# One step order for loads, stores and bias tiles in a two-layer mixing kernel

## The reference, cut to what matters

```
rel  = tril(row - col);  nd = log(|c*rel| + 1) / (log(|c*max(rel_max, threshold)| + 1) + eps)
bias = relu(nd * W1 + b1) @ W2 + b2            # 32 hidden values -> 16 channels
y    = x + bias
out  = y @ (w + eye)                            # channels
     + rank two per row    (qw1, qw2) + rank two per column (kw1, kw2)
     + y * qdd (per row) + y * kdd (per column)
```

## Time and profile before

| | |
|---|---|
| median of three runs (lowest, highest) | 977.46 us (973.42, 980.99) |
| profiled execution: time, span | 958.2 us, 956.4 us |
| mean granted TensorE clock | 0.913 |
| PE busy | 751.1 us (79%) |
| DVE busy | 451.8 us (47%) |
| ACT busy, without its DMA issues | 386.0 us (40%) |
| POOL busy | 369.8 us (39%) |
| DMA, packets' time as share of 16 engines: q1 (SyncE), q10 (ScalarE) | 41.5%, 30.9% |
| moved | 149.64 MB, mean 156 GB/s |

### The profile page before, as it was taken

The page is one execution under the profiler, slowest core; times in us unless marked ns, Lnnn a source line. Parts: engine busy times, 40 slices in busy tenths (PEclk is TensorE's granted clock), DMA queues, the critical chain, the costliest instruction groups (busy, mean ns, idle before and its releaser), DMA issues.

```text
span 956.4 us, 39070 instructions
## 1 busy us (share of the span) xinstructions
PE 751.1 (79%) x18210; PEld 551.5 (58%) x18210; DVE 451.8 (47%) x482; ACT 386.0 (40%) x412; POOL 369.8 (39%) x204
## 2 busy tenths in 40 slices
PE   0687465897779857879899989987979679997972
PEld 0255344675657545656557656756557456766972
DVE  7495332375336533456336534553336334662342
ACT  3969223543545415633434335332433334431200
POOL 4545212232223312326456637553446445650000
PEclk9879777899889987989999989998899899998997
DMA  6785587838982999378964998399835996297089
GB/s 135 178 173 106 123 155 159 193 80 202 233 186 58 216 161 196 91 143 188 249 139 82 231 204 177 62 210 187 188 77 112 234 218 149 54 202 148 5 188 168
DMA packets 364286, 149.64 MB, mean 156 GB/s; under 512 B 97372, under 2 KB 363996, under 8 KB 364124
## 3 DMA queue, kind: packets, MB, share of 16 engines
q1 hardware_dynamic: 226528, 80.00, 41.5%
q10 hardware_dynamic: 137596, 67.14, 30.9%
HBM read 77.61 MB, written 69.47 MB: 154 GB/s over the span
## 4 chain that ended last, share of the span: by engine, by line
PE 54%; SPq 14%; DMA 9%; issue 8%; ACTq 6%; DVE 4%; ACT 4%; POOL 0%; DVEq 0%
PE main L679 22%; PE main L668 18%; PE bias L693 14%; SPq L296 9%; DMA mats_a<-a_mats 7%; SPq L287 5%; ACTq L239 5%; DMA homes<-in_x 2%; ACT homes L440 1%; ACT hidden L429 1%; DVE homes L260 1%; ACT homes L456 1%; DVE homes L574 1%; DMA out_mixed<-homes 1%; DVE w_blocks L549 1%
## 5 line engine op out<-in xcount | busy, mean ns | idle before, releaser
L393 POOL TENSOR_TENSOR hidden<-log_table,row_scale 128x1024 f32<-128x1024 f32 x192 | 365.7, 1919 | 486.8 <-PE bias L693 481.1
L679 PE MATMUL main<-homes,mats_b 32*32 32x120 f32 (+1 forms) x9216 | 283.7, 272 | 84.0 <-issue 59.8
L429 ACT ACTIVATE hidden<-hidden,b_col 128x1024 f32<-128x1024 f32 x192 | 219.0, 1148 | 316.6 <-issue 156.4
L679 PEld LDWEIGHTS main<-homes,mats_b 32*32 32x32 f32 x9216 | 256.5, 133 | 151.4 <-issue 113.8
L668 PE MATMUL main<-homes,mats_a 32*32 32x128 f32 x8192 | 267.5, 280 | 63.1 <-DMA mats_a<-a_mats 35.2
L668 PEld LDWEIGHTS main<-homes,mats_a 32*32 32x32 f32 x8192 | 242.3, 131 | 124.1 <-issue 79.2
L592 DVE SCALAR_TENSOR_TENSOR homes<-bias,b_col,homes 64x512 f32<-64x512 f32 (+1 forms) x256 | 185.9, 747 | 134.1 <-PE bias L693 84.9
L693 PE MATMUL bias<-hidden,w_blocks 128*64 128x512 f32 x768 | 211.0, 655 | 24.8 <-ACT hidden L429 15.3
L574 DVE TENSOR_TENSOR homes<-main,homes 128x1024 f32<-128x1024 f32 x128 | 156.8, 1225 | 137.2 <-PE main L668 134.6
L564 DVE COPY homes<-main 128x960 f32<-128x960 f32 x64 | 74.1, 1158 | 211.2 <-PE main L679 211.1
L456 ACT ACTIVATE homes<-main 128x960 f32<-128x960 f32 (+1 forms) x80 | 71.0, 890 | 136.6 <-PE main L679 118.1
(11 more groups left out here) (36 smaller groups left out, 30.1 us busy)
## 6 DMA issues: line engine op xcount, KB each, us to landing
out_mixed<-homes ACTq DMA_DIRECT2D x208, 192.0 KB
homes<-in_x SPq DMA_DIRECT2D x200, 192.0 KB, 6.5
homes<-in_x SPq DMA_DIRECT2D x72, 256.0 KB, 7.1
out_mixed<-homes ACTq DMA_DIRECT2D x64, 256.0 KB
out_mixed<-homes ACTq DMA_DIRECT2D x72, 128.0 KB, 4.5
homes<-in_x SPq DMA_DIRECT2D x136, 64.0 KB
mats_a<-a_mats SPq DMA_DIRECT2D x256, 32.0 KB
b_mats<-homes SPq DMA_DIRECT2D x2, 512.0 KB, 3.4
```

The source lines that it names most:

```text
L393: nc.gpsimd.tensor_tensor(hidden_tile(u, g).rearrange("p (j s) -> p j s", j=ROWS), bass.AP(logs.tensor, logs.offset, [list(logs.ap[0]), [1 ...
L429: nc.scalar.activation(hidden_tile(u, g), hidden_tile(u, g), ACT.Relu, bias=b1_col[:, 0:1])\
L679: mm = pe.matmul(main[of_group(g), i % 2, j * W:j * W + REGION_TILES[k] * ROWS], b_weights(g, C * ROWS + j), y_column(k, g, C * ROWS + j), ...
```

## The change

Four things change together; the work and its data are the same.

- Stores go two blocks a step, four steps a piece (`store_share`, `store_start`, `stores_at`): steps 2 to 5, 6 to 9, 10 to 13, 14 to 17 and 18 to 21, counted from the row stage's first; the last two pieces reach steps 0 to 6 of the next column stage. In the last region it is four blocks a step, two steps a piece.
- Loads of region k + 2's pieces 0 to 4 go two blocks a step from steps 8, 12, 16, 20 and 24 of region k, counted in the same way (`LOAD_STEPS`, `loads_at`), so that 14 of their 40 DMAs lie in the row stage and 26 in the next column stage (before 24 and 16). Piece 5 of region k + 1 goes in two halves at row steps 8 and 9 (6 and 7 in region 0). The wait for the slots stands once a piece (`wait_slots`).
- SyncE's list now runs over steps. A chunk of row matrices comes one step later in it, with the same wait; in the steps of the column stage nothing in it waits for TensorE.
- Bias tile T of the next region comes at step 3 + T * 26 // 14 instead of 1 + 2 * T (for regions of 15), and ScalarE adds the constant half of tile T - 1 at the bias tile T.

```diff
-PORTIONS = (3, 3, 2)
+STORE_SHARE = 2
+LOAD_SHARE = 2
+LAST_LOAD_STEP = {8: 6, 15: 8}
+LOAD_STEPS = (8, 12, 16, 20, 24)
...
-            return 1 + T * (COL_TILES + REGION_TILES[k] - 3) // (REGION_TILES[k + 1] - 1)
+            return 3 + T * (COL_TILES + REGION_TILES[k] - 5) // (REGION_TILES[k + 1] - 1)
...
+        def blocks_of(part, share):
+            return BLOCK_ORDER[part * share:(part + 1) * share]
+
+        def store_share(k):
+
+            return STORE_SHARE if k + 1 < REGIONS else BLOCKS // 2
+
+        def store_start(k, i):
+
+            ready = piece_start(store_pieces(k), i + 1)
+            return ready if i == 0 else max(ready, store_start(k, i - 1) + BLOCKS // store_share(k))
+
+        def since_rows(r, k, s):
+
+            return s - COL_TILES + (COL_TILES + REGION_TILES[r] if k == r + 1 else 0)
+
+        def stores_at(k, s):
+
+            found = []
+            for r in (k - 1, k):
+                if r >= 0:
+                    for i in range(len(store_pieces(r))):
+                        part = since_rows(r, k, s) - store_start(r, i)
+                        if 0 <= part < BLOCKS // store_share(r):
+                            found.append((r, i, part))
+            return found
+
+        def loads_at(k, s):
+
+            found = []
+            for r in (k + 1, k + 2):
+                if 2 <= r < REGIONS:
+                    for i, start in enumerate(LOAD_STEPS):
+                        part = since_rows(r - 2, k, s) - start
+                        if 0 <= part < BLOCKS // LOAD_SHARE:
+                            found.append((r, i, part))
+            return found
...
-                while k + 1 < REGIONS and loaded[k + 1] < 5:
-                    load_x(k + 1, loaded[k + 1])
-                    loaded[k + 1] += 1
...
-                for T in range(REGION_TILES[k]):
-                    v, last = divmod(tile_of(k, T), CHUNK_TILES)
-                    if last == CHUNK_TILES - 1 and v + A_RING < CHUNKS:
-                        load_mats_a(v + A_RING)
-                    if k + 1 < REGIONS and T == min(6, REGION_TILES[k] - 4):
-                        load_x(k + 1, 5)
-                    if k + 2 < REGIONS and T in (7, 10, 13):
-                        load_x(k + 2, loaded[k + 2])
-                        loaded[k + 2] += 1
+                for s in steps(k):
+                    T = s - COL_TILES
+                    if T > 0 or (s == 0 and k):
+                        v, last = divmod(tile_of(k, max(T, 0)) - 1, CHUNK_TILES)
+                        if last == CHUNK_TILES - 1 and v + A_RING < CHUNKS:
+                            load_mats_a(v + A_RING)
+                    if k + 1 < REGIONS and T in (LAST_LOAD_STEP[REGION_TILES[k]], LAST_LOAD_STEP[REGION_TILES[k]] + 1):
+                        part = T - LAST_LOAD_STEP[REGION_TILES[k]]
+                        if part == 0:
+                            wait_slots(k + 1, 5)
+                        load_x(k + 1, 5, blocks_of(part, BLOCKS // 2))
+                    for r, i, part in loads_at(k, s):
+                        if part == 0:
+                            wait_slots(r, i)
+                        load_x(r, i, blocks_of(part, LOAD_SHARE))
...
-                    for r, i, p in portions_at(k, s):
-                        if p == 0:
+                    for r, i, part in stores_at(k, s):
+                        if part == 0:
...
-                        add_const_bias(k + 1, T)
...
+                        if T:
+                            add_const_bias(k + 1, T - 1)
+                        if T + 1 == REGION_TILES[k + 1]:
+                            add_const_bias(k + 1, T)
```

More of the change, by code:

```diff
@@ L239, in store_block @@
             return eng.dma_start(out[0, :, t0:t0 + n, b * W:(b + 1) * W], home_rows(b, mixed_slot(k, T), n))
-        def portion_blocks(p):
-            return BLOCK_ORDER[sum(PORTIONS[:p]):sum(PORTIONS[:p + 1])]
-        def portions_at(k, s):
-            found = []
[L247 to L253, removed]
+        def blocks_of(part, share):
[8 more added lines that the diff above has]
+        def stores_at(k, s):
+            found = []
+            for r in (k - 1, k):
[13 more added lines that the diff above has]
+                            found.append((r, i, part))
             return found
@@ L275, in load_compact, with wait_slots @@
                              vd.rearrange("o (b p) g m -> p (o b) (g m)", p=P)).then_inc(weights_in[part], DMA)
-            def load_x(k, i):
+            def wait_slots(k, i):
                 T, n = piece_start(load_pieces(k), i), load_pieces(k)[i]
@@ L284, in load_x @@
                     sp.wait_ge(out_done[left], times(STORE_PIECES, left, k - 2) * PER_PIECE)
+            def load_x(k, i, blocks):
+                T, n = piece_start(load_pieces(k), i), load_pieces(k)[i] * ROWS
                 t0 = tile_of(k, T) * ROWS
-                for b in BLOCK_ORDER:
-                    sp.dma_start(home_rows(b, x_slot(k, T), n * ROWS),
-                                 x[0, :, t0:t0 + n * ROWS, b * W:(b + 1) * W]).then_inc(x_in[i], DMA)
+                for b in blocks:
+                    sp.dma_start(home_rows(b, x_slot(k, T), n),
+                                 x[0, :, t0:t0 + n, b * W:(b + 1) * W]).then_inc(x_in[i], DMA)
             def load_mats_a(v):
@@ L317, in _ @@
             load_compact("b", kw1, kw2, kdd)
-            load_x(0, 0)
+            load_x(0, 0, BLOCK_ORDER)
             load_compact("a", qw1, qw2, qdd)
             sp.dma_start(w_eye, w.rearrange("g m n -> g (m n)").partition_broadcast(P)).then_inc(weights_in["a"], DMA)
-            load_x(0, 1)
-            load_x(0, 2)
+            load_x(0, 1, BLOCK_ORDER)
+            load_x(0, 2, BLOCK_ORDER)
             save_mats("b")
@@ L327, in _ @@
             for i in range(3):
-                load_x(1, i)
+                load_x(1, i, BLOCK_ORDER)
             save_mats("a")
-            load_x(1, 3)
+            load_x(1, 3, BLOCK_ORDER)
             sp.wait_ge(mats_out["a"], 2 * DMA)
@@ L333, in _ @@
                 load_mats_a(v)
-            load_x(1, 4)
+            load_x(1, 4, BLOCK_ORDER)
             sp.wait_ge(tables_made, 3)
             sp.dma_start(late_scales, scale_late).then_inc(scales_out, DMA)
-            loaded = [3, 5] + [0] * (REGIONS - 2)
             for k in range(REGIONS):
-                while k + 1 < REGIONS and loaded[k + 1] < 5:
-                    load_x(k + 1, loaded[k + 1])
-                    loaded[k + 1] += 1
                 if k == 2:
@@ L469, in _ @@
                 for s in steps(k):
-                    for r, i, p in portions_at(k, s):
-                        if p == 0:
+                    for r, i, part in stores_at(k, s):
+                        if part == 0:
                             taken, count = emptied(a_tile(r, piece_start(store_pieces(r), i + 1) - 1))
                             act.wait_ge(taken, count)
-                        for b in portion_blocks(p):
+                        for b in blocks_of(part, store_share(r)):
                             store_block(act, r, i, b).then_inc(out_done[i], DMA)
@@ L483, in _ @@
                             make_hidden(tile_of(k + 1, T + 1))
-                        add_const_bias(k + 1, T)
[L485 to L489, removed]
+                        if T:
+                            add_const_bias(k + 1, T - 1)
+                        if T + 1 == REGION_TILES[k + 1]:
+                            add_const_bias(k + 1, T)
+            last = REGIONS - 1
+            for i in range(len(store_pieces(last))):
+                for part in range(BLOCKS // store_share(last)):
+                    if store_start(last, i) + part >= REGION_TILES[last]:
+                        if part == 0:
+                            taken, count = emptied(a_tile(last, piece_start(store_pieces(last), i + 1) - 1))
                             act.wait_ge(taken, count)
-                        for b in portion_blocks(p):
-                            store_block(act, REGIONS - 1, i, b).then_inc(out_done[i], DMA)
+                        for b in blocks_of(part, store_share(last)):
+                            store_block(act, last, i, b).then_inc(out_done[i], DMA)
         @block.vector
```

## The result

The changed kernel is slower: 981.16 us, median of 20 runs (968.32 to 996.59), against 966.15 us for the kernel before (20 runs, 946.14 to 980.99); the ratio is 1.020 (1.014 to 1.026). I had forecast 957 from 977, a ratio of 0.979. Executions of one kernel fall in a faster and a slower group: the ratio compares the faster groups alone, which is why it is not the quotient of the two medians (1.016), and the profiled execution of the changed kernel is one of the slower ones. It took 987.59 us, 6 above its median, so I read it for where time moved and leave the amount to the ratio.

What follows compares the result with a forecast made beforehand. The kernel was taken to alternate between TensorE and full DMA engines, with row matrices waiting for SyncE. Terms -24 and +3 gave -21 on the profiled 958.2 us, so 937, or 957 against the runs' median 977.46; range 925 to 990.

Steps and rivals of the forecast that it cites:

- rival B: First seven column steps, regions 2 to 8: ScalarE's 14 stores ahead of its copies bound them; +38, 994 us; chance 0.19.
- Order of SyncE in the row stage: Row stages of regions 2, 3, 5, 6: fewer loads ahead of late chunks, shorter TensorE waits for matrices; -24 us.
- every chunk would start within 2 us of its slot: SyncE's row-matrix chunks: sign that the forecast holds, each started within 2 us of its slot coming free.
- Piece 5 later: Region ends: the next region's last x tile leaves behind a chunk, delaying regions 1 and 2; +3 us, bounds 0 and +20.
- Stores at nothing: Column steps 0 to 6: ScalarE's fourteen stores just fit in 22.4 us, cost nothing; 65 us if the cover is gone.
- SyncE's column loads at nothing: Column stages: up to 16 loads move from the full first half into the second; 0, between -5 and +5 a region.
- Bias tiles at 0: Bias tiles two steps later, constant half one bias tile later: +3 and -3 cancel; 0 us, bounds -8 and +8.
- C: Column stages: spread loads and stores halve the 59.8 us of "issue" waits before matmuls; -30 more, 927 us; chance 0.18.
- D: Row stage: SyncE falls behind anyway, two chunks stay late, half of the 24 us remains; 968 us; chance 0.11.
- My own sign that the prediction is wrong: First-half column stretches: the prediction is wrong if TensorE's change there by more than 5 us a region.

Runs made afterwards that it cites:

- loads_alone: The kernel before with only SyncE's new load order, stores and bias tiles as before; ratio to the kernel before 0.985 (0.978 to 0.992).
- dry_columns: The changed kernel with column-stage stores and regions 3 to 8's loads of pieces 1 to 4 moving one row each; ratio to the kernel before 0.902.
- bias_alone: The kernel before with only the bias tiles two steps later, constant half one bias tile later; ratio to the kernel before 1.009 (1.004 to 1.015).
- stores_alone: The kernel before with only the new store schedule, two blocks a step; ratio to the kernel before 1.020 (1.015 to 1.025).

## Why the prediction was wrong, point by point

The forecast was a ratio of 0.979 and the measured one is 1.020. That 981 us lies in the stated range, 925 to 990, is no merit of the sum: the range reached that far for rival B.

- **Order of SyncE in the row stage, -24.** Right in kind, high in size. The waits named for regions 2, 3 and 5 are gone and region 6's fell from 5.72 to 1.84 (35.2 to 16.8 in all, forecast 16). The chunk of region 2 started at 323.76, forecast 322.2. In regions 2 to 8 the waits for matrices fell by 19.3 us (forecast 19.1) and TensorE was busy 4.9 us less (forecast 4.8), but its other idle time rose by some 7, so the rows gained 16.9; in loads_alone 19.8. The forecast that every chunk would start within 2 us of its slot did not hold: it is 3.6 us in region 2, 6.5 in region 4, 3.4 in region 7.
- **Piece 5 later, +3.** Right in sum, 3.2. The wait before region 1's columns went from 8.26 us to 10.44; the second part came in region 6 (0 to 0.98) and not in region 2 as worked out.
- **Stores at nothing, SyncE's column loads at nothing.** These two are the steps that failed: the column stages grew by 50.4 us, 7.2 a region, where I had 0 for both (for the loads at most 5 a region, for the stores 65 us in all, but only if ScalarE's issues no longer fitted). Timed alone the stores cost 2.0%, some 19 us, by longer pauses; the loads lengthened the columns by 23 us, 3.2 a region, by waits for x, which ate the 20 us that their order gained in the rows. I asked whether ScalarE could afford fourteen issues, found 21.8 us within 22.4, and so let them pass for free. It could: a store cost it 1.08 us on average in the column stages, less than the 1.31 before. What I did not add up is bytes. The earlier trace rows had the DMA share at 1.03 and 0.97 in the first half, and the change moved 13 MB into that stage with the remark that bytes there hardly change. The Trainium skill's rule that I cited (DMA: Bandwidth & Descriptors, Issuing engines are not separate DMA queues) speaks of shared engines; the windows agree: the full half stayed at share 1.00 and took 35.6 us instead of 28.5. I had used it to say that nothing changes there.
- **Who pays for full queues.** I had listed "issue", 59.8 us, as nothing that the profile shows. In the column stages nearly all of it is instruction packets that come late, and its growth was the largest single loss of the change. The Trainium skill (Runtime: NRT & Kernel Launch, Instruction fetch mechanics) says that instructions come in blocks of 16 KiB by a DMA queue, and that crossing a block is mostly hidden. The packets of this trace agree on the size; on the cost the measurement decides: hidden for the most part in dry_columns (9 us of pauses in seven column stages), pauses of up to 6.0 us with full queues.
- **Bias tiles at 0.** The shift alone cost 0.9%, some 9 us, at the edge of the bounds of 8 us. VectorE's wait for piece 1 is not its doing: in the column stages VectorE waits for x 78 us in loads_alone, with the bias tiles where they were, and 4 in bias_alone. It belongs to the loads, and I had not costed it.
- **Rival B** had the side and the place (slower, first column steps; 994 us against 981) and the wrong mechanism: TensorE had no wait for ScalarE's copies there. That its number came near is luck. **C** asked whether "issue" would halve; it rose by 35 us. **D** did not occur. My own sign that the prediction is wrong, first halves off by more than 5 us a region, came true: 221 against 184 us in sum over seven regions, 5.3 each.

## What to carry to other kernels

Before work is moved between stages, add up the bytes of each stage and read the DMA share there; transfers moved into a stage whose engines are full can cost their time even when every issue fits. A pause of TensorE in the middle of a run of matmuls, with no semaphore and about every 255 records, is a sign that its instructions wait behind data; look whether a q8 packet ends just before it resumes. And when a change has three parts, time each alone: here one gained 1.5%, one cost 2.0% and one 0.9%, and only the whole had been forecast.

## What the runs showed of the hardware

By the profile's DMA table and the count of records, TensorE's instructions travel as DMA packets on a queue of their own, q8, 16 KB (255 instructions on average) a packet. In 51 of 52 long pauses a matmul resumed 1.2 to 1.7 us after such a packet had ended. In this kernel a packet lasts for two 32 x 32 tiles and a bias group, 3.51 and 1.08 us in dry_columns, so TensorE depends on the next one every 4 to 5 us. Its pauses in seven column stages were 79 us at 70 MB, 51 at 56 MB and 9 at 9 MB, though not in proportion in the kernels between (40 at 61 MB, 61 at 54 MB).

A full DMA share does not fix the rate: region 2's first half moved 236 GB/s at 1.03 before, 210 at 1.00 after the change and 178 at 1.02 in stores_alone. A DMA issue took ScalarE 1.08 us on average in the changed kernel's column stages, 0.72 when the same 91 stores moved a third; whether the smaller transfer or the emptier queues did it is not separated.
